# Four small-head attentions: raw head groups copied out, and keys and values of the cross layers made in a lane of their own

## The reference, cut to what matters

```
layer 0:  x += MHA(ln1 x, ln1 x, 16 heads of 64); x += MHA(ln2 x, ctx, 16 heads of 64); x += GEGLU(ln3 x)
layer 1:  x = ln(one-head attention(ln(x Wt), ln(ctx Wa), ctx Wa) Wo + x)
layer 2:  x += MHA(ln1 x, ln1 x, 16 heads of 8);  x += MHA(ln2 x, ctx, 16 heads of 8);  x += MLP(ln3 x)
layer 3:  q = unit(rope(rms(x) Wq)); k = unit(rope(ctx Wk)); v = ctx Wv
          x += softmax(q k^T sqrt(8)) v Wo            # 16 heads of 8

MHA:      softmax(q k^T / sqrt(d)) v Wo + bo
```

## Time and profile before

| | us |
|---|---|
| median of 3 runs | 2418.36 |
| lowest, highest | 2410.45, 2421.84 |
| the profiled execution | 2416.31 |
| its span, first to last instruction | 2414.4 |
| PE, DVE, ACT, POOL busy | 1911.6, 1490.4, 1372.0, 232.1 |

### The profile page before, as it was taken

How to read it: one execution, slowest core, us unless ns; L and a number is a source line. 1 busy time by engine, 2 the same in 40 slices (tenths; PEclk the granted TensorE clock), 3 DMA queues, 4 the chain that set the end, 5 groups by cost and what they waited for, 6 DMA issues and landing times. The chain is left out here.

```text
span 2414.4 us, 40394 instructions
## 1 busy us (share of the span) xinstructions
PE 1911.6 (79%) x13984; PEld 1481.5 (61%) x13984; DVE 1490.4 (62%) x3423; ACT 1372.0 (57%) x3562; POOL 232.1 (10%) x488
## 2 busy tenths in 40 slices
PE   1899886777689987677768998778768898867877
PEld 1677665555577766555557776566546776655654
DVE  2667567774367665677446766577745675667763
ACT  1556555766455554566645555466655555446765
POOL 0000012111100001111100000111020000011111
PEclk6999998988899998898889999889899999989989
DMA  4000000000000000000000000000000000000000
GB/s 128 7 1 1 1 1 1 1 1 1 18 1 1 1 1 1 1 1 1 1 17 1 1 1 1 1 1 1 1 9 9 1 1 1 1 1 1 1 1 5
DMA packets 24159, 13.75 MB, mean 6 GB/s; under 512 B 9264, under 2 KB 23472, under 8 KB 23952
## 3 DMA queue, kind: packets, MB, share of 16 engines
q1 hardware_dynamic: 23952, 11.05, 1.8%
HBM read 9.99 MB, written 1.05 MB: 5 GB/s over the span
## 5 line engine op out<-in xcount | busy, mean ns | idle before, releaser
L1013 ACT ACTIVATE probs<-scores,nmax 128x512 f32<-128x512 f32 (+1 forms) x1024 | 587.3, 579 | 170.4 <-DVE nmax L1437 168.4
L1437 DVE TENSOR_REDUCE nmax<-scores 128x1 f32<-128x512 f32 (+1 forms) x768 | 520.0, 684 | 122.6 <-PE scores L406 71.9
L474 PE MATMUL turned<-ident,probs 128*128 128x128 f32 x3072 | 499.1, 287 | 75.1 <-ACT probs L1013 73.0
L474 PEld LDWEIGHTS turned<-ident,probs 128*128 128x128 f32 x3072 | 380.0, 147 | 167.2 <-ACT probs L1013 121.5
L783 PE MATMUL heads_out<-probs_t,v 128*32 128x256 f32 (+1 forms) x4096 | 383.2, 415 | 7.9 <-issue 4.0
L852 ACT ACTIVATE probs_t<-turned 128x512 f32<-128x512 f32 x384 | 229.4, 597 | 101.6 <-PE turned L474 95.5
L1450 DVE COPY probs_t<-turned 128x512 f32<-128x512 f32 x384 | 262.0, 682 | 25.4 <-PE turned L474 25.0
L783 PEld LDWEIGHTS heads_out<-probs_t,v 128*32 128x32 f32 (+1 forms) x4096 | 185.9, 127 | 135.8 <-issue 53.8
L737 PE MATMUL scores<-k_t,q_mask 128*128 128x256 f32 (+1 forms) x512 | 193.8, 427 | 75.5 <-POOL q_mask L1566 37.1
L1462 DVE TENSOR_TENSOR out_t<-heads_out,scale_t 128x256 f32<-128x256 f32 x192 | 81.6, 425 | 271.7 <-ACT scale_t L852 271.7
L1566 POOL CAST q_mask<-q_t 32x256 fp32r<-32x256 f32 x384 | 159.3, 415 | 645.4 <-PE scores L737 223.8
(11 more groups left out here) (312 smaller groups left out, 3322.5 us busy)
## 6 DMA issues: line engine op xcount, KB each, us to landing
out_t<-ctx_dram SPq DMA_DIRECT2D x8, 192.0 KB, 2.6
v<-wqt_dram SPq DMA_DIRECT2D x2, 512.0 KB, 4.9
wo<-wo_dram SPq DMA_DIRECT2D x2, 512.0 KB, 5.6
x<-x_dram SPq DMA_DIRECT2D x8, 128.0 KB, 2.5
y_dram<-x SPq DMA_DIRECT2D x8, 128.0 KB, 1.8
v<-wkt_dram SPq DMA_DIRECT2D x1, 512.0 KB, 5.0
probs_t<-wv_dram SPq DMA_DIRECT2D x1, 512.0 KB, 6.3
wff<-wff_dram SPq DMA_DIRECT2D x1, 512.0 KB, 5.6
```

What stands on the lines that cost most here:

```text
L474: return nc.tensor.transpose(out, in_, ident[:, :])
L1013: last = nc.scalar.activation(probs[:, n % 3, k * S:k * S + ph.keys], bank[:, k * S:k * S + ph.keys], ACT.Exp, bias=nmax[:, h * QB + qb:h ...
L1437: nc.vector.tensor_reduce(out, src, AX.X, ALU.max, negate=True).then_inc(sem["attention_max"], 1)
```

## The change

1. `self2` and `cross2` no longer normalise group by group. The exponentials are made without a sum; values get a column of ones (`v_heads`, 9 columns, not padded to 32), and a group is copied out raw by DVE (`out_of_bank`, `quad_copy`). Reciprocals, `rinv`, its two transposes and `scale_copy` go.
2. `mid2` and `mid3` begin as `end` does: two transposes of four blocks (`t0`, `t1`), reciprocal and product on DVE, transpose back (`nat_t`, a copy on ACT), and a projection of two products instead of eight.
3. A step list can now have several *lanes* beside a phase (`planned` merges them by due unit). A second lane makes keys and values of the cross layers one phase before they are transposed: `keys2` beside `self2`, `keys3` beside `cross2`. Values are copied by ACT straight from the bank, the bias of `keys2` comes from a row of ones in `ctx_hi`, and the rotated keys of `keys3` get their length from a power on POOL, in four instructions, instead of from the square root and reciprocal.
4. The second copy of the high part (`queries_twice`, `keys_twice`) moves from ACT to POOL, as do the clears of the pads. The four key transposes of `mid2` and `mid3` (`kt0` to `kt3`) move to earlier steps, all through `queries_m` and all copied by ACT, with weights of 0.3 that put two into one unit or into neighbouring ones.
5. In `mid1` and `mid3` the steps of the gate and of the first MLP product are joined to the step before.

```diff
+        turned = 0 if self.masked else self.groups
         return {"t": t, "t_hi": t, "t_lo": t, "mask": H if self.masked else 0, "scores": banks,
                 "max": self.units * qm, "exp": banks, "turned": self.units * qm,
-                "copied0": self.units // 2 * qm, "copied1": self.units // 2 * qm, "rinv": self.groups * qm,
-                "heads": self.groups, "scale": self.groups * qm, "out_scaled": self.groups}
+                "copied0": self.units // 2 * qm, "copied1": self.units // 2 * qm, "rinv": turned,
+                "heads": self.groups, "scale": turned, "out_scaled": self.groups}
...
-    "mid2": "wo stats hat kv0 kv1 m2_t msplit q high low qt0 qt1 kt0 kt1 kt2 kt3",
-    "mid3": "wo stats hat m3_t up down squares rmshat kv0 kv1 krope rms_t rsplit q qrope root unit high "
-            "low qt0 qt1 kt0 kt1 kt2 kt3",
+    "keys2": "kv0 kv1",
+    "mid2": "t0 t1 nat_t wo kt0 kt1 stats hat kt2 kt3 m2_t msplit q high low qt0 qt1",
+    "keys3": "kv0 kv1 krope pow0 pow1 pow2 pow3 kunit khigh",
+    "mid3": "t0 t1 nat_t wo kt0 kt1 stats hat m3_t down kt2 squares kt3 rmshat rms_t rsplit q qrope root unit high "
+            "low qt0 qt1",
...
+PAIR = [("self0", 0, [[("start", 1)]]), ("self0", 1, [[("mid0", 0)]]), ("cross0", 0, [[("mid0", 1)]]),
+        ("cross0", 1, [[("mid1", 0)]]), ("self2", 0, [[("mid1", 1)], [("keys2", 0)]]),
+        ("self2", 1, [[("mid2", 0)], [("keys2", 1)]]), ("cross2", 0, [[("mid2", 1)], [("keys3", 0)]]),
+        ("cross2", 1, [[("mid3", 0)], [("keys3", 1)]]), ("l3", 0, [[("mid3", 1)]])]
...
-    spare = content in ("g1", "l1", "s1", "p1", "qkv1", "up1", "kv1", "qt1", "kt1", "kt3", "t1")
+    spare = content in ("g1", "l1", "s1", "p1", "qkv1", "up1", "kv1", "qt1", "kt1", "t1")
+    if chain in ("mid2", "mid3"):
+        spare = spare or content in ("kt0", "kt1", "kt2", "kt3")
...
+def planned(lanes, units):
+    steps = []
+    for lane in lanes:
+        steps += due([(name, s, step) for name, s in lane for step in STEPS[name].split()], units)
+    return sorted(steps, key=lambda at: at[0])
...
+    ("mid2", 0): {"kt0": 0.3, "kt1": 0.3, "kt2": 0.3, "kt3": 0.3},
+    ("mid2", 1): {"kt0": 0.3, "kt1": 0.3, "kt2": 0.3, "kt3": 0.3},
+    ("mid3", 0): {"kt0": 0.3, "kt1": 0.3, "kt2": 0.3, "kt3": 0.3, "m3_t": 2},
+    ("mid3", 1): {"kt0": 0.3, "kt1": 0.3, "kt2": 0.3, "kt3": 0.3, "m3_t": 2},
+    ("keys2", 0): {"kv0": 3},
+    ("keys2", 1): {"kv0": 3},
...
+            def turn_heads(chain, s, phase):
+                for qb in range(QB):
+                    yield f"t{qb}"
+                    key = chain, s, f"t{qb}"
+                    fill_bank(key)
+                    for g in range(QUADS):
+                        if qb == 0:
+                            pe.wait_ge(sem["attention_out_scaled"], PHASES[phase, s].at("out_scaled", g + 1))
+                        last = transpose(bank_of(key)[:, g * P:(g + 1) * P], outs(s, g)[:, qb * P:(qb + 1) * P])
+                    last.then_inc(sem[filled(key)], 1)
+                yield "nat_t"
+                for content in ("t0", "t1"):
+                    pe.wait_ge(sem[bank_read((chain, s, content))], FILL[chain, s, content])
+                turn_tokens((chain, s, "nat_t"), heads_nat, QB)
+                yield "wo"
+                pe.wait_ge(sem[bank_read((chain, s, "nat_t"))], FILL[chain, s, "nat_t"])
+                project_out(chain, s, "wo", 1, out_t[s][:, QUADS:QUADS + 1, :], lambda j: wo_heads[chain][:, :])
...
+                        stationary = v_heads[ph.name][s][:, kb, h, :] if ph.masked else v0[s][:, kb, h * E0:(h + 1) * E0]
+                        rows = slice(w * i, w * i + (E2 + 1 if ph.masked else w))
...
-                if not ph.key_major:
+                if not ph.masked:
                     pe.wait_ge(sem["attention_rinv"], ph.at("rinv", g + 1))
...
-            def stack_high(chain, s, kb_count):
-
-                act.wait_ge(sem["natural"], each_layer(s, chain))
-                copy(f32r(q_stack[s][:, :, :, 0:8]), heads4(nat_q[:, :, :]))
-                keys = heads4(nat_kv[:, 0:kb_count, 0:D])
-                copy(f32r(k_stack[s][:, 0:kb_count, :, 0:8]), keys).then_inc(sem["high_once"], 1)
-                copy(f32r(q_stack[s][:, :, :, 8:16]), heads4(nat_q[:, :, :]))
-                copy(f32r(k_stack[s][:, 0:kb_count, :, 16:24]), keys).then_inc(sem["high"], 1)
-                if chain == "mid1":
-                    act.wait_ge(sem["pads"], nth("pads", s, 2))
-                copy(v_pad[s][:, 0:kb_count, :, 0:8],
-                     heads4(nat_kv[:, 0:kb_count, D:2 * D])).then_inc(sem["v_padded"], 1)
-
-            def turned_stacks(chain, s, kb_count):
-
+            def queries_high(chain, s):
+                copy(f32r(q_stack[s][:, :, :, 0:8]), heads4(nat_q[:, :, :])).then_inc(sem[f"{chain}_q_high"], 1)
+
+            def keys_high(chain, s, kb_count):
+                copy(f32r(k_stack[s][:, 0:kb_count, :, 0:8]), heads4(nat_k[s][:, 0:kb_count, :])
+                     ).then_inc(sem[f"{chain}_k_high"], 1)
+
+            def values(chain, s, r, phase):
+                act.wait_ge(sem[filled((chain, s, f"kv{r}"))], FILL[chain, s, f"kv{r}"])
+                bank = bank_of((chain, s, f"kv{r}"))[:, :].rearrange("p (b n) -> p b n", b=2)
+                return bank, copy(v_heads[phase][s][:, 2 * r:2 * r + 2, :, 0:E2], heads4(bank[:, :, D:2 * D]))
...
+                elif name == "keys2":
+                    for r in range(2):
+                        yield f"kv{r}"
+                        bank, _ = values(name, s, r, "cross2")
+                        copy(f32r(k_stack[s][:, 2 * r:2 * r + 2, :, 0:8]), heads4(bank[:, :, 0:D])
+                             ).then_inc(sem["keys2_k_high"], 1)
...
+                    out, src = probs[:, n % 3, k * S:k * S + ph.keys], bank[:, k * S:k * S + ph.keys]
+                    shift = nmax[:, h * QB + qb:h * QB + qb + 1]
+                    if ph.masked:
+                        last = nc.scalar.activation(out, src, ACT.Exp, bias=shift)
+                    else:
+                        last = nc.scalar.activation(out, src, ACT.Exp, bias=shift, accum_out=sums[:, qb, h:h + 1])
...
+                    yield "krope"
+                    for r in range(2):
+                        key = name, s, f"kv{r}"
+                        dve.wait_ge(sem[bank_read(key)], FILL[key])
+                    rotate(heads4(nat_k[s][:, :, :]), TB, k_squares[:, :, :])
+                    nc.vector.tensor_scalar(k_squares[:, :, :], k_squares[:, :, :], EPS_L2 ** 2, None, ALU.max
+                                            ).then_inc(sem["keys3_squares"], 1)
+                    yield "kunit"
+                    dve.wait_ge(sem["keys3_pow"], TB * rank(s, name) + TB)
+                    unit_length(heads4(nat_k[s][:, :, :]), TB, k_norm[:, :, :]).then_inc(sem["keys3_keys"], 1)
+                    yield "khigh"
+                    keys_low(name, s, TB)
...
+            def out_of_bank(ph, g):
+                if ph.masked:
+                    quad_copy(ph, g)
+                else:
+                    scale_out(ph, g)
...
+            def settled(but=""):
+                for name, count in issued.items():
+                    if name != but:
+                        pool.wait_ge(sem[name], count)
...
+            def queries_twice(chain, s):
+                settled()
+                pool.wait_ge(sem[f"{chain}_q_high"], rank(s, chain) + 1)
+                signal(nc.gpsimd.tensor_copy(f32r(q_stack[s][:, :, :, 8:16]), q_stack[s][:, :, :, 0:8]),
+                       f"{chain}_q_twice")
+
+            def keys_twice(chain, s, at, blocks):
+                settled()
+                pool.wait_ge(sem[f"{chain}_k_high"], at)
+                signal(nc.gpsimd.tensor_copy(f32r(k_stack[s][:, blocks, :, 16:24]), k_stack[s][:, blocks, :, 0:8]),
+                       f"{chain}_k_twice")
...
+                    for kb in range(TB):
+                        yield f"pow{kb}"
+                        settled()
+                        pool.wait_ge(sem["keys3_squares"], rank(s, name) + 1)
+                        signal(nc.gpsimd.tensor_tensor(k_norm[:, kb, :], k_squares[:, kb, :], minus_half[:, :], ALU.pow),
+                               "keys3_pow")
+                    yield "khigh"
+                    keys_twice(name, s, rank(s, name) + 1, slice(0, TB))
```

557 lines of the change are left out of this document (302 added, 255 removed), and 2 rows, old and new, of tables (CHAINS, STEPS).

## The result

The changed kernel takes 2446.2 us (median of 4 runs, 2433.1 to 2454.9), the kernel before, run beside it, 2415.6: a ratio of 1.0127, 95% interval 1.0089 to 1.0165. It is 1.3% slower, where 4% faster was forecast, 2322 us with a range up to 2404. The profiled execution took 2433.1 us with a span of 2431.3, 17 us more than the span of the kernel before.

What follows compares the result with a forecast made beforehand. No engine fills the stages; engines in written order waiting for each other bound them. Savings 74, 16, 26, 14, 12 and costs 19, 13, 16 summed to -94 us: from 2416.3 to 2322 us, range 2262 to 2404.

Steps and rivals of the forecast that it cites:

- group ends: At 64 group ends in self2 and cross2, dropping normalisation saves 1.15 us each, 74 us; bounds 31 and 132.
- sums: 512 exponentials lose the accumulator read, 0.18 us each on ACT; 16 us of 92 counted; bounds 0 and 92.
- stack: PE's 51 us of waits for the keys' low part: half saved, 26 us; bounds 0 and 51.
- keys out of mid3: In l3 s0, the keys' work leaves the long chain: 14 us saved; bounds 0 and 21.
- DVE in cross2: In the cross2 stages DVE has net 18 us less work: 12 us saved; bounds 0 and 18.
- cost (b): At some 12 places paired key transposes share a unit and bank queries_m, PE waiting for ACT: 13 us cost.
- (a): Unit 0 of 16 second-lane stages: kv0 shares a bank with t0 or mid1's projection, 1.2 us each, 19 us cost.
- (c): POOL's 32 powers of 16 columns, 2.9 us each, mostly hidden by its lead: 16 us cost; bounds 0 and 93.
- The rival "slower": POOL becomes the bound of the cross2 stages, powers standing among masks: +61 us, 2477 us; chance 9%.
- what would show it wrong: PE's q_mask waits growing by tens of us, cross2 s0 getting longer, or one unit-0 wait of several us.
- a lock on the port shared by both: DVE operations with two SBUF inputs stand still during POOL powers: 1 us in each of 8 stages, sum 8 higher.

Runs made afterwards that it cites:

- wide_ends: wide_masks with the sums, inverse sums, scale_t and product of self2 and cross2's masked attentions put back: 2401.9 us, ratio 0.9932.
- wide_sums: wide_masks with only the sums put back in the 512 exponentials, read by nobody, group ends still raw: 2355.7 us, ratio 0.9744.
- kv0_late: Changed kernel with the second lane's kv0 moved out of unit 0 in 12 of 16 places, t0 staying there: 2418.3 us, ratio 1.0004.
- wide_kv0: wide_masks with the second lane's kv0 moved away from t0 in 12 of 16 places, as in kv0_late: 2312.0 us, ratio 0.9558.
- short_pow2: Changed kernel with the 32 POOL powers of 16 columns replaced by copies of constants (wrong lengths of l3's keys): 2411.1 us, ratio 0.9966.
- wide_short: wide_masks with the 32 powers replaced by short copies, as in short_pow2: 2333.4 us, ratio 0.9655.
- wide_masks: Changed kernel with eight q_mask places instead of four, so POOL makes each mask four heads earlier: 2341.9 us, ratio 0.9686.
- before_wide: Kernel before the change with eight places for masks instead of four, the new ones in t_hi and t_lo: 2397.7 us, ratio 0.9925.
- mid2_late: Changed kernel with mid2's lane begun two units later in self2 s1 and four later in cross2 s0: 2403.6 us, ratio 0.9934.
- keys2_back: Changed kernel with lane keys2 put ahead of mid2's steps, a stage later, instead of beside mid1 and mid2: 2395.0 us, ratio 0.9896.

## Why the prediction was wrong

It had 2416 - 94 = 2322, and 2446 came. The errors, term by term, in us over the whole run; a difference of two medians is known to some 5 us:

| term | predicted | measured | by |
|---|---|---|---|
| group ends | -74 | -46 | wide_ends less wide_sums |
| sums | -16 | -14 | wide_sums |
| stack, keys out of mid3, DVE in cross2, cost (b) | -39 | about -42 | remainder with early masks, not measured alone |
| (a) kv0 behind t0, 16 places | +19 | about +38 | 12 places at 2.3 to 2.5 on average (kv0_late, wide_kv0), 16 at the same price; not the bank alone |
| (c) powers | +16 | +35; +8 with early masks | short_pow2; wide_short |
| masks late, apart from (c) | 0 | the rest of +82 | wide_masks less before_wide |

With the masks early on both sides -46 - 14 - 42 + 38 + 8 = -56, the -42 being what is left over; the prediction had -94: 28 us of that miss are the group ends, 19 term (a), and 2 the sums, less 8 for the powers and 3 for the remainder. Then come the 82 us of the masks. -56 + 82 is +26, and +30 was measured.

**The step that failed** is (c): "POOL may run three heads ahead of the scores, six units of 1.2 to 1.6 us, so all but the first of each four should be hidden; I take 0.5 us each, 16 us". The length was right (2898 ns in this profile, 2.9 was the estimate), and so was the count: 8 of 32 powers lie under a wait of PE for the scores of self2 and cross2. What failed is the lead of three heads, and with it that the rest of POOL's order is priced at nothing. The three heads are what the places in q_mask allow. What the written order leaves is another thing: a mask stands three units ahead of its scores in POOL's program, in cross2 one head and a half, and a step of the chain in the same unit stands ahead of it with its wait. When POOL has waited at `stats` until DVE comes to that unit, little or nothing is left of these three units: in cross2 s0 PE ran out 0.4 us after the variance was there, in the kernel before 0.7 us ahead of it. So a power right behind that step is paid in full, 2.9 us. The trace of before had the sign of it: POOL's 223.8 us of waits for PE's scores were the lead, and PE's 37.1 us for q_mask, with waits of up to 4.4 us, told that it was already spent at 12 places. The other half of the step is what was not listed: 56 copies of the high parts, with 292 us of waits for ACT, ahead of masks. In place of 16 us the masks cost 82, of which the powers' length is 35 less 8.

The rival "slower" had the right mechanism, POOL ahead of the masks, and the right place, the cross2 stages; but it decided by the length of a power, with a turning point of 3.4 us with no cover. The powers cost only 1.1 to 1.7 us each; the order around them did the rest. Of the signs named under what would show it wrong, two came true: PE's waits for q_mask grew by tens of us and cross2 s0 got longer.

**Group ends.** 1.15 us for each of 64 was forecast, 46 / 64 = 0.72 came. The copy to scale_t is gone, and DVE now waits for PE instead, in the second round in the four stages, beside the 5.2, 5.1, 7.0 and 7.9 us of the earlier trace rows:

```profile
DVE out_t L1562 <- PE heads_out L826: 1.6, 3, 0.9
...
DVE out_t L1562 <- PE heads_out L826: 3.0, 3, 2.0
...
DVE out_t L1562 <- PE heads_out L826: 4.7, 2, 3.1
...
DVE out_t L1562 <- PE heads_out L826: 9.7, 4, 3.5
```

19.0 us instead of 25.2, 1.2 us for each group end instead of 1.6, where 0.9 was forecast. In self2 s0 little is left of the wait, in cross2 s1 it has even grown. Part of it is the masks: in wide_masks the four stages have 1.4, 1.6, 3.3 and 6.2 us, 0.8 for each group end, as forecast. So the waits came as foreseen once the masks were early, and the time did not: what DVE is freed of at a group end is not all on the path. Which wait takes its place was not looked into.

**Sums.** The term was right and its working was not. Four exponentials of 256 columns in a row, after:

```profile
1013.02 1.56 ACT L1089 ACTIVATE probs<-scores,nmax 128x256 f32<-128x256 f32 x4
```

(1.56 - 0.48) / 3 = 0.36 us from start to start, against 0.46 with the sum and a forecast of 0.28, which was taken from a copy. (One takes 0.48 by the groups, and they overlap.) So the read costs 0.10 us and not 0.18, some 51 us of ACT in all if those of 512 columns cost the same, of which 14 were on the path. Two errors met.

**Stack step.** The waits of PE for low parts were 51.3 us; at L1251, the queries' low part, 2.0 us are left, and at L1256, the keys', none. The waits went as forecast; what that is worth in time was not measured alone. The stages of self2 s1 (35.3 us in the second round, forecast 32) and l3 s0 (45.1, forecast 43) went the way that was forecast, and with the masks early they reach 32.1 and 41.0 in wide_masks.

## What to carry to other kernels

Where an engine that works in written order serves the bound one, here POOL with its masks, price each added instruction by what is left of the lead at that place, after the waits around it, and not by its length against the lead that the buffers allow. Look in the profile whether the engine waits for its consumer (lead left) or the consumer for it (lead spent), and at which places. If the lead is spent, more places help more than shorter instructions: here eight masks instead of four gave 104 us and the powers' whole length 35. When a step is moved beside another that uses the same bank, its own work counts as well as the wait, as soon as the next work of the bound engines stands behind it. And before a gain is put down to a wait, look whether that wait fell: mid2_late and keys2_back gained 43 and 51 us and left PE's waits for masks nearly as they were. wide_late, with the change, eight places, kv0 out of unit 0 and the later mid2, takes 2309 us, 4.4% less than the kernel before.

## What the runs showed of the hardware

**A POOL power does not hold up DVE, a POOL cast does.** The prediction weighed a lock on the port shared by both, held for a whole POOL instruction. In cross2 s0 of the changed kernel an addition with two SBUF inputs runs inside a power:

```profile
1063.74 0.43 DVE L1234 TENSOR_TENSOR x<-x,row_boca 128x256 f32<-128x256 f32 x1
```

It takes 0.43 us, as alone, while the power of 2.90 us that started at 1062.41 (above) is running; so it was in all 8 additions of a row that met a power (424 to 427 ns). The same form beside three masks in a row:

```profile
962.45 0.61 DVE L1234 TENSOR_TENSOR x<-x,row_bout 128x256 f32<-128x256 f32 x1
```

```profile
961.94 1.39 POOL L1718 CAST q_mask<-q_t 32x256 fp32r<-32x256 f32 x3
```

0.18 us more, about half of a cast, which takes 0.39 us where it meets none of these additions. The Trainium skill, page "SBUF — State Buffer", section "Who interferes with whom", has the lock for the whole instruction; the cast agrees with that as far as it goes, the power does not, and the 8 us that the prediction worked out from that rule are not seen in these rows. Whether the 8.5 us of wide_short are anything of this kind stays open.

**The clock was lower in the kernel that stalls, and not only behind the stalls.** The work of cross2 s0 was done at a granted clock of 1.00 before, which is the higher level, 2.4 GHz, throughout; in the changed kernel at 0.87, a part of it at the lower level of 1.2 GHz; in wide_masks at 1.00 again in the same round, with nearly the same instructions. In the changed kernel the first stretch at the lower level began ahead of PE's 4.0 us for a mask. Four transposes that take 0.60 us at the higher level:

```profile
1055.35 1.05 PE L499 MATMUL turned<-ident,probs 128*128 128x128 f32 x4
```

Just before, PE had stood 2.3 us for ACT's copy of keys. In wide_masks it stood as long at the same step (to 1029.63), and the same four transposes at 1030.36 took 0.60 us. So what brought the clock down there is not shown; the two later stretches of this stage at the lower level, from 1079 and from 1093 on, each came behind a wait for a mask. From 1055.3 to 1065.5 the granted clock was 0.50. The mean time of a scores product is 428 ns in the changed kernel and 405 in wide_masks. So part of the 82 us is the clock; how much was not separated, nor what of it the waits for masks brought about.

```profile
L779 PE MATMUL scores<-k_t,q_mask 128*128 128x256 f32 (+1 forms) x512 | 194.7, 428 | 93.7 <-POOL q_mask L1718 74.1
```

```profile
L779 PE MATMUL scores<-k_t,q_mask 128*128 128x256 f32 (+1 forms) x512 | 183.7, 405 | 10.8 <-DVE k_t L1427 6.6
```
